# Per-engine step orders for attention and mLSTM, bfloat16 maxima written by their own reductions, and two additions taken from two tensors, in a three-stage decoder layer

## The chip, the cores and the metric

The kernel runs on one core of one Trainium2 chip. The metric is the device time of one execution in microseconds (us). The profile is of one execution.

## The reference, cut to what matters

Sixteen sequences of 256 positions and 256 features go through three pre-norm sub-layers, each with a residual:

```python
x = x + attn(layernorm(x), W_qkv, W_out)      # 16 heads of 16, causal softmax; W_out enters only as a sum per head
x = x + mlstm(layernorm(x), ctx, ctx, ...)    # 8 heads of 32; gates from [q, k, v]; log-sigmoid cumulative sums
x = x + moe(layernorm(x), router, up, down)   # 8 experts of 1024, two per token, exact GELU
```

The softmax subtracts a row maximum, `exp(s - m)`. Any m that is the same for a whole row gives the same result, so m may be rounded. mLSTM computes `S = (q k^T / sqrt(32)) * exp(log_d - max)`, then `S v`, divides by a normalizer, and takes a root-mean-square norm per head.

## The kernel before

Three stages follow each other: attention over 16 batches (to about 320 us), mLSTM over 16 batches (to about 550 us), and the experts in 71 tiles of 128 tokens (to the end). All synchronization is by semaphores. Each engine runs one in-order stream of instructions, written by its own function (`tensor_attn`, `vector_attn`, `scalar_attn`, `gpsimd_attn`, `sync_attn`, and the same five for mLSTM). SyncE (SP) issues nearly all DMAs, in order, and a wait in front of one DMA holds all later ones.

**Attention.** One generator, `attn_steps`, gives all five engines the same list of named steps. In round i it works on several batches at once. In the order of TensorE: S1(i,0) (scores of the upper query half, 4 heads at a time, for the maxima), T0(i-1,0) (transposed scores minus the maximum, for the softmax), PV(i-2), S1(i,1), QK(i+1) (projection of queries and keys), T0(i-1,1), S0(i), VX(i) (values of batch i and transposes of the attention output of i-3), T2(i-1), A4(i-2) (transposes of the output), AX(i) (transposes of the normalized rows: of i+2 for attention and of i-4 for mLSTM's queries), MG(i) (transposes of the maxima, and the gate sums of i-5). VectorE's parts: `tensor_reduce` over each PSUM pair for the maxima (L1049, L1054), Mp (L1062 and L1064: the float32 maxima `mxn` split into a bfloat16 high part and a bfloat16 rest), A4 (L1073 to L1077), AX (L1085 the low part of the mLSTM queries, L1090 the low part of xn), MG (L1103, the gate sums). ScalarE's parts: exponentials of T0 (L1354) and T2 (L1360), the copies of QK (L1372 to L1374), A6c (L1419, the context's high part), AX (L1430, L1391), MG (L1395, the transposed maxima). GpSimd's: the causal selects (L1548), the layer norm's power of -0.5 (L1522), the weight splits (L1531, L1533: a float32 chunk in `STG` is split into two bfloat16 parts), and A6c (L1579).

PSUM is used as four pairs of banks, given out in TensorE's order: a step waits until the step four places before it has been read out (`pair_free`). So T0's two halves wait for the read-outs of AX and MG, S1's second half for that of A4, S0's second half for that of QK.

The weight chunks: SyncE loads two 128x512 chunks in each round into the two buffers of `STG`, GpSimd splits them. A load waits for the split of the chunk two before it. In SyncE's list a round has loads, A4 (output rows to `o_scr`, then a wait until they have landed, then the load `Mm` from there), AX (`q_scr`, and the next context `CnT`).

In round 15 ScalarE also works on the gates of batches 0 to 7 (GT: a load of another activation table, two copies, a logarithm), VectorE scans them (Gs) and splits them (Gp), and SyncE stores them (Go), loads queries, and loads `LR` (decays), with which mLSTM starts.

**mLSTM.** Here each engine already has its own order, the strings of `ORDER`, in words `kind:lag:unit`: in round i the step is done for batch i-lag. D (decay exponents) and S (scores) come in three units; VectorE's S (L1159) multiplies the two, after ScalarE's exponential (L1439). PV multiplies by the values. B3 to B6, B4x, B5s, B5n, B4o normalize, add the residual, take the third layer norm, and compute router logits (L890); R1 to R6 route two batches together. `rest` are the attention's steps of the last batches and the second half of the gates. ScalarE and GpSimd also split two weight chunks in a round (L1450, L1586), and `sc` are GpSimd's indirect DMAs that scatter rows (L1610). TensorE's B6 shares a PSUM bank with B4, and waits until VectorE's B4 (L1185 to L1188) has read it.

Two small VectorE operations take a constant as an immediate: L1004, variance plus 1e-5 in every layer norm, and L1212, `8 - KM` in R2.

Of the kernel before, what the change touches and what calls it, by code (L numbers as in the profile page):

```python
# [31 lines left out]
C_ID, C_MASK, C_U, C_SEL, C_M0, C_M1, C_TOK, C_EK, C_J, C_DUMP, C_RB, C_S0, C_IN, C_DN, C_END = (  # L32
    0, 128, 256, 384, 416, 417, 418, 450, 458, 529, 530, 538, 540, 544, 552)
# [40 lines left out]
def attn_steps():  # L74


    for i in range(-2, B + 1):
        if ok(i):
            yield "load", 2 * i, 0
            yield "load", 2 * i + 1, 0  # L80
            yield "S1", i, 0
        if ok(i - 1):
            yield "T0", i - 1, 0
        if ok(i - 2):
            yield "PV", i - 2, 0
        if ok(i + 2):
            yield "A0s", i + 2, 0
        if ok(i):
            yield "S1", i, 1
            yield "split", 2 * i, 0  # L90
        if ok(i + 2):
            yield "A0n", i + 2, 0
        if ok(i + 1):
            yield "QK", i + 1, 0
        if i == B:
            yield "queries", 0, 0
            yield "Gp", 0, 0
            yield "Go", 0, 0
            yield "decays", 0, 0
        if ok(i - 4):  # L100
            yield "A6s", i - 4, 0
        if i == -2:
            yield "weights", 0, 0
        if ok(i - 1):
            yield "T0", i - 1, 1
        if ok(i):
            yield "S0", i, 0
            yield "split", 2 * i + 1, 0
        if ok(i) or ok(i - 3):
            yield "VX", i, 0  # L110
        if ok(i - 4):
            yield "A6n", i - 4, 0
        if ok(i - 1):
            yield "T2", i - 1, 0
        if ok(i):
            yield "Mp", i, 0
        if i == B - 1:
            yield "GT", 0, 0
        if ok(i - 4):
            yield "A6c", i - 4, 0  # L120
        if ok(i - 2):
            yield "A4", i - 2, 0
        if i == B - 1:
            yield "Gs", 0, 0
        if ok(i + 2) or ok(i - 4):
            yield "AX", i, 0
        if ok(i) or ok(i - 5):
            yield "MG", i, 0
        if i == 13:
            yield "Gt", 0, 0  # L130
        if i == -1:
            yield "weights", 1, 0
        if i == 0:
            yield "weights", 2, 0
# [20 lines left out]
def weight_chunks():  # L155
# [19 lines left out]
}  # L175


def entries(engine):

    for word in ORDER[engine].split():  # L180
        kind, lag, *u = word.split(":")
        yield kind, int(lag), int(u[0]) if u else 0


def mlstm_steps(engine):
# [60 lines left out]
def build(nc, x, ctx_in, ctx_t, wqkv, wout, wg, bg, gain, wr, br, wup, wdn, cst, out):  # L246
# [6 lines left out]
    with st:  # L253
# [56 lines left out]
        mxn = sb("mxn", [128, 2, 2, 4, 2], F32, ca)  # L310
# [23 lines left out]
        Mph = Mp[:, :, :, :, 0:4].rearrange("p t a j (r h) -> p (t a j) r h", h=2)  # L334
        mxv = mxn[:, :, :, :, :].rearrange("p t a j r -> p (t a j) r")
# [42 lines left out]
        steps = list(attn_steps())  # L378
# [27 lines left out]
        lns = [s[:2] for s in steps + dve_steps if s[0] in ("A0s", "A6s", "B5s")]  # L406
# [8 lines left out]
        qk = of(steps, "QK")  # L415
        qkm, q_, ke_, ko_ = (sig(n, qk) for n in ("qkm", "q_", "ke_", "ko_"))
        vmm, v_ = sig("vmm", [(b,) for b in range(B)]), sig("v_", [(b,) for b in range(B)])
        s1 = [(b, P, u) for b, P in of(steps, "S1") for u in range(2)]
        s1m, mx1 = sig("s1m", s1), sig("mx1", s1)
        s0 = [(b, u) for b, _ in of(steps, "S0") for u in range(2)]  # L420
        s0m, mx0 = sig("s0m", s0), sig("mx0", s0)
        each = [(b,) for b in range(B)]
        mp_, mpT, mt_ = (sig(n, each) for n in ("mp_", "mpT", "mt_"))
        t0m, ex0, pt0 = (sig(n, [(b, P, u) for b, P in of(steps, "T0") for u in range(2)]) for n in ("t0m", "ex0", "pt0"))
        t2m, ex2, pt2 = (sig(n, [(b, u) for b, _ in of(steps, "T2") for u in range(2)]) for n in ("t2m", "ex2", "pt2"))
# [8 lines left out]
        for kind, b, P in steps:  # L434
# [183 lines left out]
        def tensor_attn(e, w):  # L618
            for kind, b, P in steps:
# [370 lines left out]
        def ln_stats(e, w, kind, b):  # L990
# [13 lines left out]
            e.tensor_scalar(mv[:, :, 2], mv[:, :, 1], 1e-5, None, ALU.add).then_inc(var.sem, 1)  # L1004
# [31 lines left out]
        def vector_attn(e, w):  # L1036
            for kind, b, P in steps:
# [8 lines left out]
                elif kind == "S1":  # L1046
                    for u in range(2):
                        w.wait_ge(s1m.sem, s1m.at(b, P, u))
                        e.tensor_reduce(mxn[:, 1, P, 2 * u:2 * u + 2, :], pair_of("S1", b, P, u)[:, :, :].rearrange("p j (r c) -> p j r c", r=2),  # L1049
                                        AX.X, ALU.max, negate=True).then_inc(mx1.sem, 1)  # L1050
                elif kind == "S0":
                    for u in range(2):
                        w.wait_ge(s0m.sem, s0m.at(b, u))
                        e.tensor_reduce(mxn[:, 0, :, 2 * u:2 * u + 2, :].rearrange("p a j r -> p j a r"),  # L1054
                                        pair_of("S0", b, u)[:, :, :].rearrange("p j (a r c) -> p j a r c", a=2, r=2),
                                        AX.X, ALU.max, negate=True).then_inc(mx0.sem, 1)
                elif kind == "Mp":
                    w.wait_ge(mx1.sem, mx1.at(b, 1, 1))
                    w.wait_ge(mx0.sem, mx0.at(b, 1))
                    w.wait_ge(mpT.sem, mpT.at(b - 1))  # L1060
                    w.wait_ge(p_init.sem, p_init.at("Mp0"))
                    e.tensor_copy(Mph[:, :, :, 0], mxv).then_inc(dvc.sem, dvc.up())  # L1062
                    w.wait_ge(dvc.sem, dvc.n)
                    e.tensor_tensor(Mph[:, :, :, 1], mxv, Mph[:, :, :, 0], ALU.subtract).then_inc(mp_.sem, 1)  # L1064
# [77 lines left out]
        def vector_mlstm(e, w, experts):  # L1142
# [9 lines left out]
            for kind, b, u in dve_steps:  # L1152
# [58 lines left out]
                elif kind == "R2":  # L1211
                    e.tensor_scalar(XB[:, t0:t0 + 4, 259], KM, -1.0, 8.0, ALU.mult, ALU.add)  # L1212
# [125 lines left out]
        def scalar_attn(e, w):  # L1338
            for kind, b, P in steps:
# [195 lines left out]
        def gpsimd_attn(e, w):  # L1535
# [15 lines left out]
            for kind, b, P in steps:  # L1551
# [111 lines left out]
        def sync_attn(e, w):  # L1663
# [25 lines left out]
            for kind, b, P in steps:  # L1689
# [165 lines left out]
def constants():  # L1855
# [16 lines left out]
    c[:, C_S0] = p % 32 < 2  # L1872
    c[:, C_S0 + 1] = (p % 32 == 2) | (p % 32 == 3)
# [3 lines left out]
    c[:, C_DUMP] = TOK + p  # L1877
    c[:, C_RB:C_RB + 8] = REG * np.arange(8)
# [32 lines left out]
```

## Time and profile before

| | |
|---|---|
| Median of three runs | 974.06 us (972.89 to 978.18) |
| Profiled execution | 972.35 us, span 970.6 us |
| Busy share | TensorE 91%, VectorE 63%, GpSimd 52%, ScalarE 51% |
| Mean granted TensorE clock | 0.965 of 2.4 GHz |

Lines of a timeline give the start, the length, the engine, the line, the operation with its output and inputs, how many were merged, and in brackets how long the engine had been idle and who released it. Matmuls are pipelined, so the next may begin before the end that is printed.

### The profile page before, as it was taken

To read this page: it belongs to the slowest core of one execution; us is meant where nothing else is said; L and a number is where in the kernel's file an instruction comes from. 1 tells how busy PE (TensorE), PEld (TensorE's weight loads), DVE (VectorE), ACT (ScalarE), POOL (GpSimd) and SP (SyncE) were. 2 spreads that over 40 slices of the span, in tenths; PEclk is the share of its full clock that TensorE was granted. 3 is DMA by queue.
4 is the path that set the end of the run, shared out by engine and by line. 5 is a ranking of instruction groups with operands and counts; after the bars stand their busy time and mean duration, and the time that the engine had idled before them with its cause. 6 is when DMAs were issued, how large, how long until landed. Compare 5 with 4: busy or idle time off the path is not lost.

```text
span 970.6 us, 31715 instructions
## 1 busy us (share of the span) xinstructions
PE 880.4 (91%) x11877; PEld 652.7 (67%) x11966; DVE 616.0 (63%) x1324; ACT 490.8 (51%) x839; POOL 501.4 (52%) x705
## 2 busy tenths in 40 slices
PE   4899999989997688999998998999999999999995
PEld 3566666766765445556665776878787878778783
DVE  4766776676767455679898677555555555555552
ACT  3566767767765556556664643333333333333331
POOL 2454756665665433357777677633444434444432
PEclk9899999999998988889998999999999999999998
DMA  8213343334244654355564433433232333233222
GB/s 273 66 24 88 84 112 113 80 89 140 78 88 138 131 174 146 101 160 177 186 193 134 122 73 91 99 67 51 47 51 46 53 49 51 46 51 51 46 35 23
DMA packets 133198, 92.97 MB, mean 96 GB/s; under 512 B 75712, under 2 KB 114112, under 8 KB 132928
## 3 DMA queue, kind: packets, MB, share of 16 engines
q1 hardware_dynamic: 119760, 73.10, 27.2%
q0 software_dynamic: 13296, 17.83, 11.2%
q8 instruction: 106, 1.74, 0.7%
q14 instruction: 36, 0.29, 0.1%
HBM read 54.65 MB, written 37.32 MB: 95 GB/s over the span
## 4 chain that ended last, share of the span: by engine, by line
PE 63%; DVE 11%; ACT 7%; DMA 6%; issue 4%; POOL 3%; SPq 3%; POOLq 0%; DVEq 0%; ACTq 0%
PE pair L963 19%; PE pair L977 10%; PE pair L979 7%; PE pair L665 4%; PE pair L687 3%; PE pair L701 3%; DMA o_scr<-On 3%; DMA STG<-wup_in 2%; PE pair L840 2%; PE pair L638 2%; ACT PT L1360 2%; PE pair L714 2%; PE pair L854 2%; DVE SD L1159 2%; PE pair L929 1%
## 5 line engine op out<-in xcount | busy, mean ns | idle before, releaser
L963 PE MATMUL pair<-XTs,WU 128*128 128x128 bf16 x3408 | 284.0, 219 | 7.7 <-DVE XTs L1303 4.0
L963 PEld LDWEIGHTS pair<-XTs,WU 128*128 x3408 | 237.7, 98 | 75.4 <-issue 12.2
L1637 POOL DMA_INDIRECT out_d<-XB x71 | 115.6, 1629 | 202.5 <-DVE XB L1325 168.8
L1503 ACT ACTIVATE Hf<-pair 128x512 f32<-128x512 f32 x142 | 84.9, 598 | 217.2 <-PE pair L963 217.0
L977 PE MATMUL pair<-WD,Hh 128*128 x479 | 181.1, 379 | 0.2
L1316 DVE CAST Hh<-Hf 128x512 bf16<-128x512 f32 x142 | 64.3, 453 | 164.5 <-ACT Hf L1503 160.2
L979 PE MATMUL pair<-WD,Hl 128*128 x568 | 154.8, 272 | 4.8
L1548 POOL TENSOR_SCALAR_AFFINE_SELECT PT<-PT 128x512 f32<-128x512 f32 (+1 forms) x96 | 74.7, 793 | 56.8 <-ACT PT L1354 52.0
L1318 DVE TENSOR_TENSOR Hl<-Hf,Hh 128x512 bf16<-128x512 f32 x142 | 99.7, 702 | 4.9
L1049 DVE TENSOR_REDUCE mxn<-pair 128x4 f32<-128x1024 f32 x64 | 75.2, 1216 | 27.4 <-PE pair L646 27.3
L1610 POOL DMA_INDIRECT xs_scr<-XB,WGf x64 | 68.6, 1071 | 28.2 <-issue 16.7
L665 PE MATMUL pair<-Q,K 32*128 32x128 f32 (+1 forms) x1024 | 66.3, 360 | 17.3 <-DVE Gq L1103 10.6
L1354 ACT ACTIVATE PT<-pair 128x1024 f32<-128x1024 f32 x64 | 62.2, 1029 | 37.4 <-PE pair L670 37.4
L1159 DVE TENSOR_TENSOR SD<-pair,SD 128x1024 f32<-128x1024 f32 x48 | 58.6, 1221 | 19.9 <-PE pair L840 19.8
L1439 ACT ACTIVATE SD<-pair 128x1024 f32<-128x1024 f32 x48 | 49.0, 1020 | 43.4 <-PE pair L823 43.4
L665 PEld LDWEIGHTS pair<-Q,K 32*128 32x128 f32 x1024 | 42.4, 189 | 30.9 <-ACT MT L1395 19.5
L1586 POOL TENSOR_TENSOR WD<-STG,WD 128x512 bf16<-128x512 f32 x32 | 37.5, 1182 | 43.8 <-ACT WD L1450 43.6
L1054 DVE TENSOR_REDUCE mxn<-pair 128x8 f32<-128x1024 f32 x32 | 37.7, 1219 | 32.4 <-PE pair L646 32.4
L977 PEld LDWEIGHTS pair<-WD,Hh 128*128 128x128 bf16 x568 | 55.5, 98 | 2.5 <-issue 0.8
L979 PEld LDWEIGHTS pair<-WD,Hl 128*128 128x128 bf16 x568 | 55.5, 98 | 0.1
L1510 ACT ACTIVATE yt<-pair,ix 128x256 f32<-128x256 f32 x71 | 33.7, 474 | 39.7 <-PE pair L979 39.6
L1623 POOL TENSOR_SCALAR ix<-XB,TE 128x1 f32<-128x1 f32 x55 | 52.8, 960 | 0.0
(245 smaller groups left out, 1756.5 us busy)
## 6 DMA issues: line engine op xcount, KB each, us to landing
XB<-xs_scr SPq DMA_DIRECT2D x71, 130.0 KB, 2.1
STG<-wup_in SPq DMA_DIRECT2D x32, 256.0 KB, 4.7
q_scr<-SPL SPq DMA_DIRECT2D x16, 512.0 KB, 4.2
STG<-wdn_in SPq DMA_DIRECT2D x32, 256.0 KB, 3.0
o_scr<-On SPq DMA_DIRECT2D x32, 128.0 KB, 4.1
Mm<-o_scr SPq DMA_DIRECT2D x16, 256.0 KB, 2.9
CnT<-ctxt_in SPq DMA_DIRECT2D x16, 256.0 KB, 4.5
CX<-ctx_in SPq DMA_DIRECT2D x16, 256.0 KB, 3.9
```

The costliest lines, as they stand in the source:

```text
L665: e.matmul(o, K[rows, r, par, a, k0:k0 + 128], Q[rows, r, a, 256 - wd:256], start=True, stop=False, skip_group_check=True)
L963: t = e.matmul(upb(j, k)[:, 128 * (fm % 4):128 * (fm % 4) + 128], WU[:, bass.ds(reg[j] * 4096 + off, 128)], XTs[:, r, hx, dk, :], start=n ...
L977: e.matmul(yb[r][:, 0:512], Hh[:, r, hsl], WD[:, bass.ds(reg[i] * 4096 + 512 * fk, 512)], start=fk == 0, stop=False, skip_group_check=True)
L979: t = e.matmul(yb[r][:, 0:256], Hl[:, r, hsl], WD[:, bass.ds(reg[i] * 4096 + 512 * fk, 256)], start=False, stop=fk == 7, skip_group_check= ...
L1049: e.tensor_reduce(mxn[:, 1, P, 2 * u:2 * u + 2, :], pair_of("S1", b, P, u)[:, :, :].rearrange("p j (r c) -> p j r c", r=2), AX.X, ALU.max, ...
L1159: e.tensor_tensor(SD[:, un % 3, :, :], ZS[:, :, :].rearrange("p g (a c) -> p (g a) c", a=2), SD[:, un % 3, :, :], ALU.mult).then_inc(sd_.s ...
L1316: e.tensor_copy(Hh[:, r, hs], Hf[:, r, hs]).then_inc(hhi.sem, 1)
L1318: e.tensor_tensor(Hl[:, r, hs], Hf[:, r, hs], Hh[:, r, hs], ALU.subtract).then_inc(hlo.sem, 1)
L1503: e.activation(Hf[:, r, hs], upb(j, k), ACT.Gelu).then_inc(gel.sem, 1)
L1548: e.affine_select(out=dg, in_=dg, pattern=[[0, n], [1, 128]], compare_op=ALU.is_ge, fill=0.0, base=0, channel_multiplier=-1).then_inc(done ...
L1610: e.indirect_dma_start(out=xs, out_offset=bass.IndirectOffsetOnAxis(ap=SLI[:, m % 2, k, tt:tt + 1], axis=0), in_=XB[:, 4 * m + tt, :], in_ ...
L1637: e.indirect_dma_start(out=out, out_offset=bass.IndirectOffsetOnAxis(ap=XS[:, i % NX, 256:257].bitcast(I32), axis=0), in_=Yf[:, i % NY, :] ...
```

## The change

- Attention gets orders of its own for each engine, `ROUND`, read by `attn_steps(engine)` with the words of `ORDER`. `LIMITS` gives the batches of each step.
- `mxn` and the step Mp are gone. The reductions write bfloat16 maxima straight into `Mp` (one value for each head instead of a high and a low one); VectorE's S1 waits for the transposes of the batch before, TensorE's MG for the reductions, and TensorE's PV also for the selects of T0.
- mLSTM gets new orders.
- L1004 and L1212 become `tensor_tensor` with a constant column of `CF`.

```diff
-def attn_steps():      # one list for all engines
+ROUND = {
+    "tensor": "AX:1 MG:1 S1:0:0 T0:1:0 PV:2 S1:0:1 QK:-1 T0:1:1 S0:0 VX:0 T2:1 GT:15 weights:0:2 A4:2",
+    "vector": "Gp:16 weights:-2:0 A6s:4 weights:-1:1 S1:0:1 S0:0 VX:0 A4:2 weights:0:2 MG:0 AX:0 S1:-1:0 Gs:15 A0s:-3",
+    "scalar": "PV:2 A0n:-2 QK:-1 T0:1:1 Gt:13 A6c:4 weights:-2:0 A6n:4 VX:0 T2:1 weights:-1:1 AX:0 GT:15 MG:0 T0:0:0",
+    "gpsimd": "split:0 T0:1:0 T0:1:1 split:0 GT:15 T2:1 weights:0:2 A6c:4 A0s:-3 A6s:3",
+    "sync": "GT:15 load:0 A4:3 AX:1 Go:16 queries:16 decays:16",
+}
...
 ORDER = {
-    "tensor": "D:0:0 B6:4 R4:5 PV:1:1 S:0:0 D:0:1 PV:1:2 rest:0:0 D:0:2 S:0:1 rest:0:1 B5:3 PV:0:0 rest:0:2 B4:1 S:0:2",
-    "vector": "S:0:0 rest:0:0 B5s:2 S:0:1 R2:4 rest:0:1 rest:0:2 B4:1 first:14 R3:4 S:0:2 R1:3 R5:4 R6:4 B4x:1",
-    "scalar": "D:0:0 rest:0:2 split:0 D:0:1 B3:1 rest:0:0 split:0 rest:0:1 split:0 R1:4 B5:3 D:0:2 B5n:2 B4p:1",
-    "gpsimd": "sc:0 B4p:2 sc:0 R6:5 sc:0 split:0 split:0 B5s:2 rest:0:0 rest:0:1 rest:0:2 split:0",
-    "sync": "load:0 B1:0:1 B1:-1:0 B4o:2 rest:0:2 rest:0:0 rest:0:1 row:15",
+    "tensor": "D:0:0 B6:4 R4:5 PV:1:1 S:0:0 rest:0:0 D:0:1 PV:1:2 rest:0:1 D:0:2 B5:3 S:0:1 PV:0:0 rest:0:2 B4:1 S:0:2",
+    "vector": "B4x:2 rest:0:0 S:0:0 R5:5 R6:5 rest:0:1 B5s:2 S:0:1 rest:0:2 R2:4 B4:1 first:14 R3:4 S:0:2 R1:3",
+    "scalar": "rest:0:2 split:0 B4p:2 D:0:0 B5n:3 split:0 rest:0:0 D:0:1 rest:0:1 split:0 R1:4 B3:1 B5:3 D:0:2",
+    "gpsimd": "B4p:2 rest:0:0 sc:0 R6:5 split:0 split:0 sc:0 rest:0:1 sc:0 split:0 rest:0:2 B5s:2",
+    "sync": "load:0 rest:0:2 B1:0:1 B1:-1:0 rest:0:0 B4o:2 rest:0:1 row:15",
 }
...
-            e.tensor_scalar(mv[:, :, 2], mv[:, :, 1], 1e-5, None, ALU.add)
+            e.tensor_tensor(mv[:, :, 2], mv[:, :, 1], CF[:, C_EP:C_EP + 1].broadcast_to([128, 2]), ALU.add)
...
                 elif kind == "S1":
+                    w.wait_ge(mpT.sem, mpT.at(b - 1))
                     for u in range(2):
                         w.wait_ge(s1m.sem, s1m.at(b, P, u))
-                        e.tensor_reduce(mxn[:, 1, P, 2 * u:2 * u + 2, :], ...
+                        e.tensor_reduce(Mph[:, 1, P, 2 * u:2 * u + 2, :], ...
...
-                elif kind == "Mp":
-                    e.tensor_copy(Mph[:, :, :, 0], mxv)
-                    e.tensor_tensor(Mph[:, :, :, 1], mxv, Mph[:, :, :, 0], ALU.subtract)
...
-                    e.tensor_scalar(XB[:, t0:t0 + 4, 259], KM, -1.0, 8.0, ALU.mult, ALU.add)
+                    e.tensor_tensor(XB[:, t0:t0 + 4, 259], CF[:, C_EK:C_EK + 1].broadcast_to([128, 4]), KM, ALU.subtract)
```

## Rows read from the trace of the kernel before

**Rows 1.** One stretch of mLSTM: busy us of each engine with instructions, granted clock, DMA share, GB/s.

```profile
398.00:548.00 150.00, 139.93 (x1974) 91.12 (x1974) 125.42 (x332) 90.17 (x175) 96.60 (x151) 0.93 0.53 161
```

**Rows 2.** TensorE's waits from 60 to 287 us: total us, times, longest.

```profile
PE pair L665 <- DVE Gq L1103: 9.9, 9, 1.6
PE pair L665 <- DVE xTl L1090: 1.6, 3, 1.3
```

**Rows 3.** TensorE's timeline at the end of one attention round.

```profile
211.75 0.75 PE L791 MATMUL pair<-WGs,SPL 128*128 128x16 bf16 x24
...
214.34 0.71 PE L665 MATMUL pair<-Q,K 32*128 32x256 f32 x8 [1.04 <-DVE Gq L1103]
```

**Rows 4.** VectorE's timeline in the same stretch.

```profile
209.92 1.25 DVE L1064 TENSOR_TENSOR Mp<-mxn,Mp 128x32 bf16<-128x32 f32 x1
...
212.80 0.69 DVE L1085 TENSOR_TENSOR SPL<-pair,SPL 128x512 bf16<-128x512 f32 x1 [0.45 <-ACT SPL L1430]
213.41 0.68 DVE L1090 TENSOR_TENSOR xTl<-pair,xTh 128x512 bf16<-128x512 f32 x1
```

**Rows 5.** TensorE's timeline where attention starts up.

```profile
30.78 0.67 PE L625 MATMUL pair<-OTs 128*128 128x256 f32 x2 [1.53 <-issue]
...
33.85 1.24 PE L665 MATMUL pair<-Q,K 32*128 32x256 f32 x8 [0.62 <-DVE wsq L1033]
```

**Rows 6.** The chain that ended last, from 290 us.

```profile
291.85 5.55 DMA STG<-wup_in
...
301.69 1.82 ACT PT L1360 x2
303.53 1.28 ACT L1406
...
315.54 3.16 DMA g_scr<-pp
```

**Rows 7.** SyncE's queue after the gates: issues.

```profile
311.15 0.91 SPq L1735 DMA_DIRECT2D WD<-q_scr  x1
...
314.87 1.28 SPq L1723 DMA_DIRECT2D g_scr<-pp  x2
318.77 0.34 SPq L1748 DMA_DIRECT2D LR<-g_scr  x1
```

**Rows 8.** TensorE's timeline: the first mLSTM batches and the second half of the gates.

```profile
343.20 1.08 PE L906 MATMUL pair<-CF,Mm 128*128 128x128 f32 x4 [4.98 <-DMA Mm<-o_scr]
...
380.69 1.09 PE L881 MATMUL pair<-CF,XB 128*128 128x128 f32 x4 [2.11 <-ACT r L1408]
...
416.28 0.84 PE L840 MATMUL pair<-Q 64*128 64x128 bf16 x24 [1.81 <-DVE SD L1159]
```

**Rows 9.** TensorE's waits from 400 to 550 us.

```profile
PE pair L890 <- DVE sm L1188: 3.0, 5, 1.0
PE pair L854 <- DMA CX<-ctx_in: 1.3, 1, 1.3
```

**Rows 10.** VectorE's two operations with an immediate: duration min, median, max.

```profile
L1004 DVE TENSOR_SCALAR LS<-LS x48: 168/169/2483, 5.5 to 564.5; 128x2 f32<-128x2 f32 x48
L1212 DVE TENSOR_SCALAR XB<-WGf x8: 159/1166/2806, 416.1 to 585.4; 128x4 f32<-128x4 f32 x8
```

**Rows 11.** L1212 beside GpSimd, and an operation of two tensors beside GpSimd.

```profile
486.97 2.28 POOL L1586 TENSOR_TENSOR WD<-STG,WD 128x512 bf16<-128x512 f32 x2
487.11 2.17 DVE L1212 TENSOR_SCALAR XB<-WGf 128x4 f32<-128x4 f32 x1
...
540.15 1.16 POOL L1586 TENSOR_TENSOR WD<-STG,WD 128x512 bf16<-128x512 f32 x1
540.17 1.19 DVE L1219 TENSOR_TENSOR CF<-CF 128x32 f32<-128x32 f32 x1
```

**Rows 12.** Two stretches at a lower granted clock; columns as in the first group.

```profile
380.00:398.00 18.00, 17.31 (x146) 10.93 (x148) 7.99 (x18) 7.22 (x15) 2.77 (x8) 0.53 0.30 92
469.00:472.50 3.50, 3.50 (x42) 1.47 (x38) 3.29 (x7) 0.66 (x2) 1.81 (x3) 0.56 0.65 199
```

More of the change, by code:

```diff
@@ L71, in ok @@
     return 0 <= b < B
-def attn_steps():
[L77 to L134, printed above, removed]
@@ new lines, with words, attn_steps @@
+ROUND = {
[5 rows of a table added]
+}
+LIMITS = {"S1": (0, B - 1), "T0": (0, B - 1), "PV": (0, B - 2), "A0s": (0, B - 1), "A0n": (0, B - 1), "QK": (0, B - 1), "A6s": (0, B - 4),
+          "A6n": (0, B - 4), "S0": (0, B - 1), "VX": (0, B), "T2": (0, B - 1), "A6c": (0, B - 4), "A4": (0, B - 2), "AX": (-2, B), "MG": (0, B)}
+def words(line):
+    for word in line.split():
+        kind, lag, *u = word.split(":")
+        yield kind, int(lag), int(u[0]) if u else 0
+def attn_steps(engine):
+    parts = 0
+    for i in range(-4, B + 3):
+        for kind, lag, u in words(ROUND[engine]):
+            b = i - lag
+            if kind == "load":
+                if ok(b):
+                    yield kind, 2 * b, 0
+                    yield kind, 2 * b + 1, 0
+            elif kind == "split":
+                if ok(b):
+                    yield kind, parts, 0
+                    parts += 1
+            elif kind not in LIMITS:
+                if b == 0:
+                    yield kind, u, 0
+            elif LIMITS[kind][0] <= b <= LIMITS[kind][1]:
+                yield kind, b, u
@@ L169 @@
 ORDER = {
[5 rows of a table removed]
-}
[L178 to L182, printed above, removed]
[5 rows of a table added]
+}
 def mlstm_steps(engine):
@@ L190, in mlstm_steps @@
     for i in range(B):
-        for kind, lag, u in entries(engine):
+        for kind, lag, u in words(ORDER[engine]):
             b = i - lag
@@ L376, in build @@
         Hf = sb("Hf", [128, 2, 1024], F32)
-        steps = list(attn_steps())
+        pe_attn, dve_attn, act_attn, pool_attn, sp_attn = (list(attn_steps(n)) for n in ROUND)
         pe_steps, dve_steps, act_steps, pool_steps, sp_steps = (list(mlstm_steps(n)) for n in ORDER)
@@ L403, in chunk @@
             return src[:, 512 * k:512 * k + 512], v[:, :, 0, :], v[:, :, 1, :], STG[:, c % 2, :].rearrange("p (a w) -> p a w", w=width)
-        lns = [s[:2] for s in steps + dve_steps if s[0] in ("A0s", "A6s", "B5s")]
+        lns = [s[:2] for s in dve_attn + dve_steps if s[0] in ("A0s", "A6s", "B5s")]
         LNK = {k: i % 4 for i, k in enumerate(lns)}
@@ L433, in build @@
         users = []
-        for kind, b, P in steps:
+        for kind, b, P in pe_attn:
             if kind in ("S1", "T0"):
@@ L618, in tensor_attn @@
         def tensor_attn(e, w):
-            for kind, b, P in steps:
+            for kind, b, P in pe_attn:
                 if kind == "weights" and b == 2:
@@ L1003, in ln_stats @@
             w.wait_ge(dvc.sem, dvc.n)
-            e.tensor_scalar(mv[:, :, 2], mv[:, :, 1], 1e-5, None, ALU.add).then_inc(var.sem, 1)
+            e.tensor_tensor(mv[:, :, 2], mv[:, :, 1], CF[:, C_EP:C_EP + 1].broadcast_to([128, 2]), ALU.add).then_inc(var.sem, 1)
         def vector_setup(e, w):
@@ L1036, in vector_attn @@
         def vector_attn(e, w):
-            for kind, b, P in steps:
+            for kind, b, P in dve_attn:
                 if kind == "weights":
@@ L1338, in scalar_attn @@
         def scalar_attn(e, w):
-            for kind, b, P in steps:
+            for kind, b, P in act_attn:
                 if kind == "weights" and b < 2:
@@ L1549, in causal @@
                                 channel_multiplier=-1).then_inc(done.sem, 1)
-            for kind, b, P in steps:
+            for kind, b, P in pool_attn:
                 if kind == "weights" and b == 2:
@@ L1688, in sync_attn @@
                             onesb[:, :].rearrange("p (a c) -> p a c", a=1).broadcast_to([128, 2, 128])).then_inc(l_on, 16)
-            for kind, b, P in steps:
+            for kind, b, P in sp_attn:
                 if kind == "load":
```

41 lines of the change are left out of this document (18 added, 23 removed).

## The prediction

> **What bounds the kernel now.** I read the page first: TensorE is busy for nine tenths of the span, so only its gaps, its slow stretches, and whatever lengthens them can be won. Then the windows by stage: in the long mLSTM stretch of 150 us VectorE is busy 125 and TensorE 140 [rows 1], so there VectorE is nearly a second bound. Then TensorE's waits and the timeline in front of each. In the attention rounds from 60 to 287 us there is one regular hole, in front of T0, nine times and 9.9 us in all, released by the last of VectorE's read-outs [rows 2]. The reader is to see in the timeline that TensorE has finished its gate sums at 212.50 and S1 by about 213.3, and begins T0 at 214.34 after 1.04 us of nothing [rows 3], because VectorE started L1085 only at 212.80, waiting for ScalarE, and then had two more operations to do [rows 4]. Between the stages the chain of waits is a queue: weight load, GpSimd's split, normalized rows, exponentials, table load, gates, then SyncE's issues [rows 6, 7], and TensorE ends it with a wait of 4.98 us for a DMA [rows 8]. In mLSTM it waits 3.0 us for VectorE's B4 and 1.3 for a context load [rows 9], and twice around the gates' second half [rows 8]. The expert stage is untouched.
>
> **The change part by part**, against the profiled execution of 972.35 us, which lies 1.7 below the median of the runs.
>
> *The steady attention rounds.* TensorE's cyclic order stays the same: AX and MG are only written at the head of the next round. What moves is who reads out. ScalarE does A6c before the exponentials of T2 instead of between them and AX, so L1430 comes about 0.5 us earlier, and VectorE's L1085 no longer waits for it. VectorE loses the step Mp (its second operation took 1.25 us in this round [rows 4]), but it was in front of A4, which TensorE feeds only at about 210.8, so most of that was slack. VectorE now does the gate sums first: they can begin when TensorE's end, at 212.50 [rows 3]. I give them 0.13 us (an estimate: the old order left 0.61 from L1085 to L1090, and 0.25 between the end of L1090 at 214.09 and T0, the sums among it [rows 3, 4]). Then L1085 starts at 212.63 instead of 212.80, and T0 follows after 1.54 less the 0.11 that the sums no longer take at the end: 214.06. The hole goes from 1.04 to 0.76. It doesn't close, because the three operations still stand in one row behind TensorE's gate sums. Nine holes of 0.76 instead of 9.9 us: 3.1. The one round with a wait of 1.3 for L1090 [rows 2] goes to 0.76 too, and one wait of 0.3 for a late normalized row goes with the earlier splits: **-4.0 us**. Bounds: 0, if the row is held elsewhere; -11.5, if all holes close.
>
> The reductions' bfloat16 output I cost at nothing: L1085 and L1090 write bfloat16 from PSUM in 0.69 and 0.68 us for 512 columns [rows 4], the pace of any read from PSUM there. S1's new wait for the transposes is free: they end before 212, and S1 starts behind L1090. PV's wait for the selects of T0 is free since the select of T2 comes later on the same engine.
>
> *The start.* The sum over W_out (weights 2) moves ahead of AX(0) and MG(0) on TensorE. It waits for a GpSimd memset behind two weight splits, until 30.78 [rows 5], in either order, so AX, MG and S1 now come behind it. T0 stood at 33.85 [rows 5]; I get 34.6 from a matmul group of 0.9, transposes of 0.8 and VectorE's part behind the sums. Against +0.75 stands 0.35 in the next round, where QK's copies no longer stand behind a late xn: **+0.4 us** (0 to +2).
>
> *The end of attention.* SyncE now issues round i's loads in front of A4(i-2), not behind its output DMA, and GpSimd does the norm's power ahead of the splits. In round 15 the load of 5.55 us began at 291.85 and held the split, then the power, the row QN and only then the exponentials at 301.69 [rows 6]. TensorE had T2 ready at 299.1, so they can start 2.6 earlier. The table load at 303.53 [rows 6] now follows AX instead of preceding it, so the logarithm gains only 1.4 to 1.8, but VectorE starts its scans at once, and the split of the gates ends at about 311.7. SyncE issues the gates first (1.3 us) and the queries then (311.15 to 314.87 before, 3.7 us) where it was the reverse [rows 7]. The gates' landing of 3.16 [rows 6] is hidden behind the queries: the first LR issue goes from 318.77 [rows 7] to 311.7 + 1.3 + 3.7 = 316.7. All of SyncE's queue behind it (A4(14), Mm, the contexts, LR of the next batch, and the Mm that TensorE waits 4.98 for [rows 8]) is back to back and shifts as one: **-2.1 us** (0 to -3).
>
> *mLSTM, the two additions.* L1212 needs 0.16 us and took up to 2.8; it took 2.17 where it began beside two of GpSimd's subtractions, together 2.28, and it ended with them. An operation of two tensors that began beside one such subtraction ended with that one: 1.19 [rows 11]. So I take 1.2 as the worst for both new additions, where L1004's worst was 2.48 and L1212's 2.81 [rows 10]. L1212 stands in front of B4, and TensorE's waits for B4 sum to 3.0 in five [rows 9]; four of them, 2.7 us, lie behind an L1212 that took 2.2 or 2.8 and are shorter than the 1.0 to 1.6 it gives back: -2.7. Behind the two longer ones TensorE's granted clock fell for a stretch such as 469.0 to 472.5, at 0.56 [rows 12]; half speed costs 0.44 of 3.5 us each, on a busy TensorE 1.5 to 1.7: -3.3.
>
> *mLSTM, the orders.* The splits now come before most of the scatter DMAs on GpSimd, so the last loads and the context behind them start earlier: the wait of 1.3 [rows 9] goes. In round 3 ScalarE does the hyperbolic tangent before D's second exponential, and TensorE has GT before D's third unit; the wait that ended at 380.69 [rows 8] is replaced by three shorter ones in front of B5 and PV, and I get PV 1.0 earlier. In round 5 VectorE's Gp, some 3.9 us, stands before S's first unit instead of behind it: the wait of 1.81 at 416.28 [rows 8] becomes one of 3.9 in front of S's second unit, partly given back: +1.0. R1's exponential ahead of B3 (0.25 us) lies in 0.5 of slack before PV. B5n behind D's first exponential frees ScalarE where it waited for GpSimd, but no TensorE wait hangs on that. Together: -2.7 - 3.3 - 1.3 - 1.0 + 1.0 = **-7.3 us** (+6 to -16; the lower end if the 18 us at a clock of 0.53 [rows 12] also return to full, which is worth 8).
>
> Sum: -4.0 + 0.4 - 2.1 - 7.3 = -13.0; 972.35 - 13.0 = 959.4, and as the median lies above the profiled execution, **960 us**.
>
> A rule that speaks against the additions: the Trainium skill, "SBUF — State Buffer", section "Who interferes with whom", says that a VectorE instruction with two SBUF inputs contends with a GpSimd instruction that reads SBUF, and that `tensor_tensor` has no 2-port mode but contends in this way. By it both new forms still wait behind GpSimd's subtraction; the trace agrees for one of them (the row with 1.19). By the rule alone nothing would be gained there, which is the second rival below.
>
> **The rivals.**
>
> *The clock comes back too.* With fewer holes around the gates' second half, the stretch of 18 us at 0.53 [rows 12] stays at full clock or halves. For it: two holes of 1.4 and 2.1 us stand right in front of it. Against it: I only shorten them to three of about 1. Worth 4 to 8: 953.
>
> *The additions gain nothing.* They have two SBUF inputs and can be held by the same subtractions, even by both of two if each new one wins; new orders also put other operations beside them. Without -2.7 and -3.3: 966.
>
> *Slower: ScalarE's first split.* It now stands ahead of B4p and D's first exponential at the head of each round, and waits for a weight chunk from a load that SyncE may issue only after GpSimd's split of two chunks before. Before, it came after D. If the chunk lands more than about 2 us after the last exponential of the round, D's first exponential, S and D's second unit all slide. For it: VectorE and TensorE have only 5 to 15% of slack there [rows 1]. Against: GpSimd splits earlier as well. At 1.5 us in each of some 12 rounds: +18 - 1, so 977.
>
> *Nothing measurable.* The holes only move: the row behind the gate sums and SyncE's queue give back what is won, and round 5's hole costs a slow stretch. 971.
>
> **How the numbers follow.** Forecast 0.48 (its own range 955 to 965), the clock too 0.18, additions without gain 0.17, nothing 0.09, slower 0.08. The range 948 to 970 reaches from the clock's lower end to the additions' upper and leaves out the last two. A measurement of this kernel can tell about 0.5%, 969.2 to 978.9. Faster is the first three, less a little for their upper edges: 0.81; the same 0.12; slower 0.07.
>
> **What would show it.** T0's hole near 0.75 with L1090 as its releaser; no 5 us of GpSimd waiting for STG in the attention rounds; exponentials of T2 in round 15 right behind TensorE; the first LR issue about 6 us earlier than 318.77 (2.1 and the rounds before); L1004 and L1212 never above 1.3; TensorE's wait for B4 gone; a wait near 4 us in front of S in round 5. Wrong would be: a hole of T0 that stays at 1.04 or vanishes, waits of ScalarE for STG in front of B4p, or more slow stretches than before.

## The result and the profile after

The changed kernel takes 949.62 us (median of four runs, 947.91 to 955.48) against 973.47 for the kernel before: a ratio of 0.9757, 95% interval 0.9728 to 0.9786. The forecast was 960 with a range of 948 to 970. The profiled execution of the changed kernel takes 950.63 us, span 948.8; of before 972.35, span 970.6. The difference of the spans, 21.8 us, is what I divide up.

The page of the changed kernel, busy time by engine, then the granted clock in 40 slices:

```profile
PE 869.4 (92%) x11877; PEld 647.8 (68%) x11966; DVE 588.0 (62%) x1292; ACT 488.6 (51%) x839; POOL 497.3 (52%) x705
...
PEclk9899999999998979999999999999999999999998
```

**The attention rounds.** TensorE's waits from 60 to 283 us, then its timeline and VectorE's at the end of the round that answers to [rows 3, 4]:

```profile
PE pair L634 <- DVE xTl L1055: 7.6, 12, 0.7
```

```profile
208.94 0.75 PE L762 MATMUL pair<-WGs,SPL 128*128 128x16 bf16 x24
...
211.22 0.71 PE L634 MATMUL pair<-Q,K 32*128 32x256 f32 x8 [0.73 <-DVE xTl L1055]
```

```profile
208.05 0.37 DVE L1038 RECIPROCAL pair<-pair 128x32 f32<-128x32 f32 x1 [1.45 <-PE pair L702]
...
209.73 0.19 DVE L1068 TENSOR_TENSOR Gq<-pair,BG 128x32 f32<-128x32 f32 x1 [0.37 <-PE pair L762]
209.84 0.68 DVE L1050 TENSOR_TENSOR SPL<-pair,SPL 128x512 bf16<-128x512 f32 x1
210.44 0.68 DVE L1055 TENSOR_TENSOR xTl<-pair,xTh 128x512 bf16<-128x512 f32 x1
```

The hole in front of T0 is 0.73 us where it was 1.04 [rows 2, 3], and the low part of xn (now L1055) ends it. From S1 of the first full round to S1 of the last (65.90 to 285.59 before, 66.28 to 281.57 after) the rounds give 4.4 us; the start costs 0.4.

**Between the stages.** The chain that ended last, and SyncE's issues:

```profile
294.49 1.92 ACT PT L1325 x2
296.41 0.54 ACT SPL L1395
296.96 1.28 ACT L1371
...
304.87 0.29 DVE pp L1098
305.18 0.62 SPq L1688
```

```profile
305.18 1.28 SPq L1688 DMA_DIRECT2D g_scr<-pp  x2
306.55 0.55 SPq L1700 DMA_DIRECT2D WD<-q_scr  x1
307.15 1.84 SPq L1702 DMA_DIRECT2D WD<-q_scr  x4
309.10 0.33 SPq L1713 DMA_DIRECT2D LR<-g_scr  x1
```

In the attention rounds GpSimd no longer waits for STG at all, where it waited 47.7 us in twelve. The STG load of 5.55 us and everything that it held [rows 6] are off the chain: the exponentials of T2 run 7.2 us earlier, the table load 6.6, the first LR issue 9.7 (318.77 [rows 7] to 309.10).

**mLSTM.** TensorE's three waits that answer to [rows 8], in order: the load Mm, the second half of the gates, and round 5. Then its waits from 390 to 535 us, for [rows 9], and R2's first operation, for [rows 10]:

```profile
334.65 1.09 PE L877 MATMUL pair<-CF,Mm 128*128 128x128 f32 x4 [5.17 <-DMA Mm<-o_scr]
...
372.24 0.63 PE L852 MATMUL pair<-CF,XB 128*128 128x128 f32 x4 [1.11 <-ACT r L1373]
...
398.46 1.46 PE L811 MATMUL pair<-Q 64*128 64x256 bf16 x12 [2.51 <-DVE SD L1124]
```

```profile
PE pair L811 <- DVE SD L1124: 5.6, 3, 2.5
PE pair L934 <- issue: 1.1, 1, 1.1
```

```profile
L975 DVE TENSOR_TENSOR LS<-LS,CF x48: 161/164/1607, 5.6 to 542.7; 128x2 f32<-128x2 f32 x48
L1177 DVE TENSOR_TENSOR XB<-CF,WGf x8: 148/151/157, 401.2 to 563.6; 128x4 f32<-128x4 f32 x8
```

No wait for B4 is left, R2's operation (L1212 before, L1177 now) never takes above 0.157 us, and the wait of the context load is gone. The windows from the end of the wait for Mm to the first expert matmul, first before, then after (us, then busy us and instructions of each engine, granted clock, DMA share, GB/s):

```profile
343.20:548.56 205.36, 189.08 (x2622) 122.13 (x2623) 156.43 (x395) 123.01 (x233) 113.98 (x181) 0.89 0.51 157
```

```profile
334.65:526.68 192.03, 177.98 (x2622) 115.93 (x2623) 146.10 (x395) 123.47 (x233) 112.53 (x181) 0.96 0.53 166
372.00:390.00 18.00, 17.22 (x244) 11.62 (x244) 11.97 (x26) 12.29 (x27) 5.11 (x11) 1.00 0.37 112
```

mLSTM takes 13.3 us less. The same 2622 matmuls are busy for 178.0 us instead of 189.1, at a mean granted clock of 0.96 instead of 0.89: 11.1 us are shorter busy time, 2.2 fewer gaps. The stretch that stood at 0.53 [rows 12] is at 1.00. In windows of 1 us, the stretches of this stage below 0.8 add up to some 44 us before (380 to 397 [rows 12] and five others) and to some 15 after (334.65 to 343, 398 to 401, 510 to 514). The account of the spans: -4.4 rounds, +0.4 start, -4.5 end of attention (the wait for Mm ends 8.55 earlier, 4.0 of it from the rounds and the start), -13.3 mLSTM, nothing in the expert stage.

### The profile page after: what moved, and what is told of

Read it like the earlier page. It is cut to its first block, busy times and chain, and to the rows that moved or that the text cites. A ratio compares the mean times of both kernels' runs of the same rounds, so it can differ in the third digit from the quotient of the medians.

```text
span 948.8 us, 31667 instructions
## 1 busy us (share of the span) xinstructions
PE 869.4 (92%) x11877; PEld 647.8 (68%) x11966; DVE 588.0 (62%) x1292; ACT 488.6 (51%) x839; POOL 497.3 (52%) x705
## 4 chain that ended last, share of the span: by engine, by line
PE 78%; DVE 8%; ACT 6%; issue 3%; DMA 2%; SPq 2%; POOL 0%; ACTq 0%; DVEq 0%; POOLq 0%
PE pair L934 19%; PE pair L948 10%; PE pair L950 7%; PE pair L634 5%; PE pair L671 5%; PE pair L657 4%; PE pair L811 3%; PE pair L607 3%; PE pair L684 2%; PE pair L825 2%; PE pair L837 2%; PE pair L900 2%; ACT SD L1404 1%; PE pair L786 1%; PE pair L861 1%
## 5 line engine op out<-in xcount | busy, mean ns | idle before, releaser
L1487 POOL TENSOR_TENSOR LS<-LS,mhalf 128x2 f32<-128x2 f32 x48 | 34.4, 716 | 95.7 <-DVE LS L975 95.3
L1022 DVE TENSOR_REDUCE Mp<-pair 128x4 bf16<-128x1024 f32 x64 | 75.2, 1216 | 13.0 <-PE pair L615 12.7
L1575 POOL DMA_INDIRECT xs_scr<-XB,WGf x64 | 66.0, 1032 | 32.4 <-issue 17.3
L1027 DVE TENSOR_REDUCE Mp<-pair 128x8 bf16<-128x1024 f32 x32 | 37.7, 1219 | 45.1 <-PE pair L615 45.1
```

The source lines that it names most:

```text
L1022: e.tensor_reduce(Mph[:, 1, P, 2 * u:2 * u + 2, :], pair_of("S1", b, P, u)[:, :, :].rearrange("p j (r c) -> p j r c", r=2), AX.X, ALU.max, ...
L1575: e.indirect_dma_start(out=xs, out_offset=bass.IndirectOffsetOnAxis(ap=SLI[:, m % 2, k, tt:tt + 1], axis=0), in_=XB[:, 4 * m + tt, :], in_ ...
```

## The experiments

Changes below are against the kernel that is named. Each kernel was timed beside the kernel before (973.81 to 975.25 us in these series), not beside the changed kernel, so a difference of 1 or 2 us from its 949.62 says nothing.

### Run 1: the additions alone, in the kernel before

```diff
-            e.tensor_scalar(mv[:, :, 2], mv[:, :, 1], 1e-5, None, ALU.add)
+            e.tensor_tensor(mv[:, :, 2], mv[:, :, 1], CF[:, C_EP:C_EP + 1].broadcast_to([128, 2]), ALU.add)
-                    e.tensor_scalar(XB[:, t0:t0 + 4, 259], KM, -1.0, 8.0, ALU.mult, ALU.add)
+                    e.tensor_tensor(XB[:, t0:t0 + 4, 259], CF[:, C_EK:C_EK + 1].broadcast_to([128, 4]), KM, ALU.subtract)
```

> The kernel before with only the two additions written as operations of two tensors, the old orders kept. My theory: L1212 gives back 1.0 to 1.6 us behind four waits for B4 (2.7 us) and two stretches at a lower granted clock go with them (3.3 us): 973.5 - 6 = 967.5 us, both operations never above 1.3 us, TensorE's waits for B4 near 0.3 us in sum. Rival (the additions gain nothing, since two SBUF inputs wait behind the same subtractions): 973.5 us, and operations that still take up to 2.8 us.

Measured: 975.92 us, ratio 1.0004 (0.998 to 1.0027). The two lines over the whole span, then R2's operation beside GpSimd's pair of subtractions:

```profile
L1004 DVE TENSOR_TENSOR LS<-LS,CF x48: 161/164/2470, 5.5 to 567.9; 128x2 f32<-128x2 f32 x48
L1212 DVE TENSOR_TENSOR XB<-CF,WGf x8: 151/1288/2793, 416.0 to 588.7; 128x4 f32<-128x4 f32 x8
```

```profile
488.11 2.33 DVE L1212 TENSOR_TENSOR XB<-CF,WGf 128x4 f32<-128x4 f32 x1
...
488.13 2.28 POOL L1586 TENSOR_TENSOR WD<-STG,WD 128x512 bf16<-128x512 f32 x2
```

The reader is to see two ends: 490.44 and 490.41. The new form is held through both subtractions as the old one was [rows 11]. The rival is right, my bound of 1.2 us was wrong, and the interval leaves no room for the 6 us.

### Run 2: the additions undone, in the changed kernel

> The changed kernel with only the two additions back as operations with an immediate. If they are worth about 6 us in the new orders too: 949.6 + 6 = 955.6 us, with some of them above 2 us and TensorE waiting for B4 behind them. If the new orders alone had put R2 away from GpSimd's subtractions, or if the old form costs nothing there: 949.6 us.

Measured: 950.81 us (946.72 to 954.82), and the immediate form of R2's operation takes 0.154 to 0.164 us. So in neither order are the additions worth anything that can be measured, and what took R2 out of its delay is an order.

### Run 3: the old mLSTM orders, in the changed kernel

> The changed kernel with the old mLSTM orders, its attention part and its two additions kept. From the two traces attention is 8.1 us shorter up to the last context load. If that is all of attention's share and the additions are worth 6 us: 973.5 - 8.1 - 6 = 959.4 us, and TensorE's long stretch at a lower granted clock around the second half of the gates is back. Rival, the orders of mLSTM gain nothing and the clock came back with the additions: about 950 us. Rival, the additions gain nothing: 965.4 us.

Measured: 967.09 us, ratio to before 0.9921 (0.9896 to 0.9946). So the new attention alone makes the kernel 6.7 us faster, and the mLSTM orders on top of it give 16.3 to 17.5 (967.09 against 950.81 of run 2 and 949.62). Windows of the same stretch of mLSTM, and of a slow part in it:

```profile
333.87:543.31 209.44, 192.32 (x2622) 125.12 (x2623) 155.06 (x395) 122.30 (x231) 113.77 (x182) 0.88 0.50 155
372.00:382.00 10.00, 8.32 (x62) 5.92 (x62) 3.43 (x10) 4.85 (x10) 2.59 (x8) 0.54 0.20 60
```

The low clock behind the gates' second half comes back with the old orders, and so do the waits for B4 (2.7 us in four) and for the context load (3.2 us). Attention's gain doesn't arrive whole: the wait for Mm ends 9.3 us earlier than in the kernel before (333.87, 343.20), but with the same orders mLSTM then takes 209.4 us where it took 205.4.

### Runs 5 to 8: which engine's order

Runs 5 to 7 take the changed kernel and put back the old `ORDER` string of one engine (run 6 those of two, TensorE and ScalarE), and run 8 puts GpSimd's new string alone into the kernel before.

```diff
# 5
-    "gpsimd": "B4p:2 rest:0:0 sc:0 R6:5 split:0 split:0 sc:0 rest:0:1 sc:0 split:0 rest:0:2 B5s:2",
+    "gpsimd": "sc:0 B4p:2 sc:0 R6:5 sc:0 split:0 split:0 B5s:2 rest:0:0 rest:0:1 rest:0:2 split:0",
# 6
-    "tensor": ... (new)     "scalar": "rest:0:2 split:0 B4p:2 D:0:0 B5n:3 split:0 rest:0:0 D:0:1 ..."
+    "tensor": ... (old)     "scalar": "D:0:0 rest:0:2 split:0 D:0:1 B3:1 rest:0:0 split:0 ... B5n:2 B4p:1"
# 7
-    "vector": "B4x:2 rest:0:0 S:0:0 R5:5 R6:5 rest:0:1 B5s:2 S:0:1 rest:0:2 R2:4 B4:1 ..."
+    "vector": "S:0:0 rest:0:0 B5s:2 S:0:1 R2:4 rest:0:1 rest:0:2 B4:1 ... R1:3 R5:4 R6:4 B4x:1"
```

> The changed kernel with GpSimd's old mLSTM order. In the profiles so far R2's small operation ends together with GpSimd's pair of weight subtractions in either form, and in the changed kernel it stands beside a scatter DMA instead. Theory: it is GpSimd's order that took it out from beside the subtractions, and the four delays of 2.2 to 2.8 us with TensorE's waits for B4 (2.7 us) and two slow stretches (3.3 us) come back: 949.6 + 6 = 955.6 us. Rival, the whole 17.5 us of the mLSTM orders hang on it: about 967 us. Rival, VectorE's or ScalarE's order did it: 949.6 us, and L1177 stays at 0.16 us.

> The changed kernel with the old mLSTM orders of TensorE and ScalarE (the second half of the gates after D's second exponential, and ScalarE's first split after D). Theory: the hole of 2.1 us and a granted clock of 0.5 for 17 us around 375 to 392 us come back, worth 1 + 8 us: 958.6 us. Rival, the clock there was chance or hangs on the other orders: about 950 us. Rival, ScalarE's early split costs: faster than 949.6 us.

> The changed kernel with VectorE's old mLSTM order (Gp behind S's first unit, R5, R6 and B4x at the end of a round, R2 one step earlier). By my prediction's term for round 5 this is 1 us better, 948.6 us, and the wait of 2.51 us in front of S's second unit becomes one near 1.8. Rival: R2 now begins beside GpSimd's work or B4 comes late behind it, and TensorE waits for VectorE again: 953 us or more.

> The kernel before with GpSimd's new mLSTM order alone. If that order is what frees R2: no R2 above 0.2 us, TensorE's waits for B4 gone, and 973.5 - 6 = 967.5 us. If what it gives elsewhere too (earlier loads, context) is most of the gain: below 962 us. If it only works with the other engines' new orders: 973.5 us.

| kernel | us | against 949.62 | R2's operation, longest |
|---|---|---|---|
| 5: GpSimd's old | 976.43 | +26.8 | 2.878 us |
| 6: TensorE's and ScalarE's old | 993.71 | +44.1 | 0.675 us |
| 7: VectorE's old | 959.19 | +9.6 | 0.159 us |
| 8: before with GpSimd's new | 986.58 (ratio 1.0117, 1.0088 to 1.0146) | | 0.681 us |

GpSimd's order does free R2 (runs 5 and 8), but nearly every number that I expected is far off: the orders aren't a sum of parts. Runs 5 and 6 are slower than all five old strings together (967.09), and run 8 is slower than the kernel before. In run 5 the rows of three engines show what is late; GpSimd, SyncE, ScalarE, and ScalarE's waits from 400 to 530 us:

```profile
455.99 2.27 POOL L1551 TENSOR_TENSOR WD<-STG,WD 128x512 bf16<-128x512 f32 x2
```

```profile
457.18 1.45 SPq L1616 DMA_DIRECT2D STG<-wdn_in  x2
```

```profile
460.88 0.63 ACT L1415 ACTIVATE WD<-STG 128x512 bf16<-128x512 f32 x1 [6.23 <-DMA STG<-wdn_in]
461.42 0.20 ACT L1426 ACTIVATE sm<-sm 128x16 f32<-128x16 f32 x1
461.65 0.22 ACT L1428 ACTIVATE sm<-sm 128x16 f32<-128x16 f32 x1
461.78 1.01 ACT L1404 ACTIVATE SD<-pair 128x1024 f32<-128x1024 f32 x1
```

```profile
ACT WD L1415 <- DMA STG<-wdn_in: 50.2, 11, 6.4
```

GpSimd's subtractions, late as in the old order, let SyncE reload the two buffers only at 457.18; ScalarE, whose split now stands first, waits 6.23 us for that chunk, and B4p and D's exponential behind it come late. From 335 to 560 us TensorE then waits 8.7 us for D's exponential, 6.4 for the copy of the normalizer's input (L1422) and 5.4 for B4, in the changed kernel 3.1, 1.3 and 0. It is the slower rival of my prediction, and in the changed kernel it is there too, as 13.3 us in eight waits (longest 4.10), which TensorE hardly notices. In run 6 it is the other way round; the waits of GpSimd and of ScalarE, 400 to 530 us:

```profile
POOL WD L1551 <- ACT WD L1415: 25.2, 14, 6.7
```

```profile
ACT XB L1300 <- POOL LS L1490: 38.1, 8, 6.3
```

GpSimd subtracts early and waits for ScalarE's high part, which is late, so its norms come late, and ScalarE waits for those: a ring. From 335 to 560 us TensorE waits 13.4 us for S and 13.2 for D's exponential (5.6 and 3.1 in the changed kernel). Run 8 shows the same pair (24.9 and 38.0 us). In run 7 TensorE waits 10.3 us in seven for S; I put that down to B4x, R5 and R6 at the end of VectorE's round, which weren't moved singly.

Run 6 also answers my question on the clock. The hole in front of the second half of the gates is back, as long as in [rows 8], and the clock behind it stays whole:

```profile
380.91 0.63 PE L852 MATMUL pair<-CF,XB 128*128 128x128 f32 x4 [2.11 <-ACT r L1373]
```

```profile
380.91:398.00 17.09, 16.98 (x238) 11.79 (x238) 11.52 (x25) 12.00 (x23) 5.41 (x14) 1.00 0.44 129
```

So that hole alone doesn't bring the stretch of [rows 12]. (Of the two holes that my prediction names there, the first is 0.60 us here, where it was 1.42.) The slow stretches of run 6 stand elsewhere (362 to 372 at 0.51, 406 to 424 at 0.53).

### Run 9: R2's operation moved, in the kernel before

```diff
# R1
                     link(e.tensor_reduce(KM, KY, AX.X, ALU.max))
+                    e.tensor_scalar(XB[:, t0:t0 + 4, 259], KM, -1.0, 8.0, ALU.mult, ALU.add)
                     link(e.tensor_tensor(O1, KY, bt(KM), ALU.is_equal))
# R2
-                    e.tensor_scalar(XB[:, t0:t0 + 4, 259], KM, -1.0, 8.0, ALU.mult, ALU.add)
```

> The kernel before with L1212 alone moved: still the form with an immediate, but at the end of R1, some 5 us earlier, where GpSimd does small operations and scatters and no weight subtraction. Theory: the delay belongs to this operation wherever it starts beside the subtractions, so it takes 0.16 us now, the later operations of R2 follow without delay, and my term of 2.7 + 3.3 us comes: 967.5 us. Rival, the next small operation of R2 (the sum at L1214) is held in its place: no change, 973.5 us. Rival, the delays vanish but were slack that TensorE takes elsewhere: 971 to 973 us.

Measured: 974.14 us, ratio 0.9971 (0.994 to 1.0001). What was L1212's place, twice: beside a pair of subtractions, and beside one.

```profile
486.24 0.18 DVE L1214 TENSOR_REDUCE WGf<-CF 128x4 f32<-128x32 f32 x1
486.33 2.72 DVE L1215 SCALAR_TENSOR_TENSOR CF<-CF 128x32 f32<-128x32 f32 x1
...
538.96 0.18 DVE L1214 TENSOR_REDUCE WGf<-CF 128x4 f32<-128x32 f32 x1 [1.45 <-ACT CF L1474]
539.06 1.03 DVE L1215 SCALAR_TENSOR_TENSOR CF<-CF 128x32 f32<-128x32 f32 x1
```

```profile
486.71 2.29 POOL L1586 TENSOR_TENSOR WD<-STG,WD 128x512 bf16<-128x512 f32 x2
...
538.89 1.16 POOL L1586 TENSOR_TENSOR WD<-STG,WD 128x512 bf16<-128x512 f32 x1 [0.16 <-ACT WD L1450]
```

The delay has only passed to another operation of R2: not to the reduction at L1214, which runs inside a subtraction in 0.18 us, but to L1215, whose two inputs are both in SBUF. It ends with the subtraction in both cases. The Trainium skill, "SBUF — State Buffer", section "Who interferes with whom", says that on this chip reductions never contend with GpSimd, and that an instruction with two SBUF inputs contends with a GpSimd instruction that reads SBUF; the trace agrees with both (0.18 and 1.03 us). My prediction cited that rule and set it aside.

### Run 10: the maxima in two parts again, in the changed kernel

The float32 `mxn` and the step Mp return, in front of VectorE's A4; TensorE's MG waits for it.

> The changed kernel with the maxima as before: float32 from the reductions, then a step on VectorE (in front of A4) that splits them into a high and a low bfloat16 part, on which TensorE's transposes wait. My prediction costed the removal of that step as slack: VectorE idles 1.45 us in front of A4, the step takes some 1.5 to 1.9 us, and 0.37 us of idle time follow behind A4: 949.6 us, hole in front of T0 still 0.73. Rival, the 4.4 us that the steady rounds gained come from this removal: 954 us and a hole near 1.0.

Measured: 950.11 us (947.09 to 955.34). From S1 of the first full round to that of the last it takes 215.3 us, as the changed kernel does, with the hole at 0.74. VectorE's idle time in front of A4 shrinks from 1.45 to 0.78 and pays for the step. So the bfloat16 maxima are worth nothing in time that can be measured, in the new order. There the step is also shorter, 0.72 us in two operations (0.49 and 0.23): in the kernel before it was 0.56 and 1.25, and the second one lay beside a subtraction of GpSimd (209.91 to 211.08) and ended 0.09 us behind it.

### Runs 4, 11 and 12: the order behind the gate sums, and two further versions

```diff
-    "vector": "... A4:2 weights:0:2 MG:0 AX:0 S1:-1:0 ..."
+    "vector": "... A4:2 weights:0:2 AX:0 MG:0 S1:-1:0 ..."
# the two later versions also: T0 and T2 on TensorE
-                    for u in range(2):
-                        pair_free(w, kind, *key, u)
+                    pair_free(w, kind, *key, 0)
...
+                            if g == 0 and j == 2:
+                                pair_free(w, kind, *key, 1)
# the last also
-    "vector": "B4x:2 rest:0:0 S:0:0 ..."
+    "vector": "B4x:2 S:0:0 rest:0:0 ..."
```

> The changed kernel with VectorE's read-outs at the end of an attention round in the old order: first the two low parts, then the gate sums. In the profile of the changed kernel the first low part can start when ScalarE's high part of the queries ends, about 0.4 us before it starts now, because it now stands behind the gate sums, which wait for TensorE. If that holds, the hole in front of T0 goes from 0.73 to about 0.45 us and the gate sums release it, in some 10 to 13 rounds: 949.6 - 3 = 946.6 us. Rival, the row is held by ScalarE's part or by TensorE's gate sums either way: hole 0.7, 949.6 us. It would also say that this piece of the change was a loss.

> The changed kernel with the low parts ahead of the gate sums on VectorE, as in the earlier run, and TensorE's T0 and T2 waiting for their second pair only in front of the third matmul. The low part of xn then ends at about 210.74 where it ended at 211.12, and T0's first half needs only that: a hole of about 0.35 instead of 0.73, in ten rounds and more: 949.6 - 4 = 945.6 us. The earlier run (hole 0.52, but 954.9 us) shows that mLSTM can give this back by slow stretches of the granted clock, so the rival is 950 to 955 us with the attention rounds 4 us shorter all the same.

> The same as the run before it, and VectorE's mLSTM order with the rest (in round 5 the split of the gates' second half, 3.9 us) behind S's first unit. By my prediction's term this takes 1 us off round 5 and perhaps the slow stretch behind the hole of 2.51 us: 944.5 us, with a hole near 1.8 at about 398 us. Rival, the rest of rounds 0 to 3 comes late behind S and mLSTM starts slower: above 946 us.

| version | us (lowest) | ratio to before | rounds, first to last S1 | hole at T0 |
|---|---|---|---|---|
| changed kernel | 949.62 (947.91) | 0.9757 (0.9728 to 0.9786) | 215.3 | 0.73 |
| run 4: low part first | 954.85 (943.57) | 0.9755 (0.9708 to 0.9803) | 213.4 | 0.52 |
| run 11: and second wait later | 951.29 (946.16) | 0.9739 (0.970 to 0.9777) | 212.5 | 0.38 |
| run 12: and gates later | 954.2 (949.81) | 0.9774 (0.9738 to 0.9811) | 212.4 | 0.38 |

Without their longest executions (957.9 and 962.48 us) the medians of runs 4 and 11 are 953.67 and 947.91. The profile of run 11 is of that longest execution, so only its attention rounds are read. T0 in the round of [rows 3], in run 4 and in run 11:

```profile
210.36 0.71 PE L634 MATMUL pair<-Q,K 32*128 32x256 f32 x8 [0.52 <-DVE Gq L1068]
```

```profile
209.88 0.75 PE L635 MATMUL pair<-Q,K 32*128 32x256 f32 x8 [0.38 <-ACT MT L1361]
```

In attention the reasons hold: doing the gate sums first, which my prediction counted as part of the gain, is a loss of 1.9 us against doing them last, since ScalarE's high part is ready before TensorE's gate sums are (209.44 and 209.69 in the changed kernel). The two changes together give 2.8. (ScalarE's MT is the next thing in the row.) But no version's time is distinguishable from the changed kernel's, because mLSTM moves by as much. In run 4, a window behind the same hole of 2.5 us as in the changed kernel, and then the changed kernel's own:

```profile
398.00:412.00 14.00, 13.89 (x116) 9.22 (x118) 7.16 (x26) 3.58 (x7) 4.33 (x9) 0.52 0.48 150
```

```profile
398.00:401.50 3.50, 3.04 (x28) 1.31 (x28) 2.94 (x10) 0.00 (x0) 1.20 (x3) 0.53 0.66 181
```

After one and the same wait the half clock (1.2 of 2.4 GHz) lasts for 3.5 us in one execution and for 14 in another. Nor does a shorter hole give a shorter stretch: in run 12 the hole is 1.10 us and 7 us at 0.53 follow (403 to 410), in run 7 it is 1.11 and 10 us at 0.51 follow (402 to 412). Executions of run 4's kernel range from 943.57 us at a mean clock of 0.984 to 957.41 at 0.969. A few us gained in attention can't be told from that with six runs.

## Why the prediction was right, and where it wasn't

**Steady rounds, -4.0: right.** 4.4 measured, hole at 0.73, released by the low part, and the maxima's split was slack, as run 10 shows. Within it, "VectorE now does the gate sums first" was no gain: by run 4 it took 1.9 back, and what else moved gave 6.3. I take that for ScalarE's earlier A6c, which no run isolates. The profiles fit it: L1430 ended 0.27 us behind TensorE's gate sums (212.77, 212.50), and its successor ends 0.25 ahead of them.

**The start, +0.4: right only as a sum.** T0 of the second batch stands at 50.79 instead of 50.41, but both terms were mis-sized: T0 of the first batch goes from 33.85 to 35.52, 1.7 later where I had 0.75, and the next round gives 1.3 back where I had 0.35. W_out's sum now waits 3.73 us in one hole instead of the shorter waits of [rows 5].

**End of attention, -2.1: right in mechanism, too small.** 4.5 measured, outside my bound of 3. "The split of the gates ends at about 311.7" was mis-sized: it ended at 314.09 before and at 305.16 now, so 4.9 us earlier apart from the 4.0 of the rounds, where I had 2.4. The exponentials begin 3.2 earlier beyond the rounds (I had 2.6) and the logarithm, and with it the scans, 2.6 (I had 1.4 to 1.8). And from the first scan to the last cast VectorE took 8.1 us before and takes 5.8 now: two read-outs (0.85) are no longer between them, and the subtraction behind the scans and two casts, which took 1.42, 0.61 and 0.75 beside GpSimd's subtraction (307.82 to 308.97) and selects (311.09 to 312.64), take 0.42, 0.28 and 0.28 with GpSimd idle. SyncE then needed 3.9 us from the gates' issue to LR, not 5.0. About 1.2 of this was given back before Mm.

**mLSTM, -7.3: the sum fell short (-13.3), and its largest term was false.** The step that failed is "So I take 1.2 as the worst for both new additions", on which -2.7 and -3.3 hung. One row beside a single subtraction told nothing about a pair of them: run 1 measures 0 (ratio 1.0004), with 2.33 to 2.79 us for the new form beside the pairs. The waits for B4 went all the same, from the orders: GpSimd does its subtractions earlier, so R2 no longer stands beside one. L975 still takes 1.61 us at worst, above the 1.3 that I named as a sign. My -1.3 for the context load held (run 3 has the wait again). Around the gates' second half the holes went from 1.42 and 2.11 us to 0.17, 1.11 and 0.44, so 1.8 less where I had 1.0. ScalarE's waits for STG in front of B4p, which I named as a sign of being wrong, did come (13.3 us, 0.9 before), without making TensorE wait as I feared. For round 5 I forecast a wait near 4 us and found 2.51; putting the gates later there cut the hole to 1.10 and gave nothing in time (run 12).

**The clock.** I took it at 3.3 us through the additions and gave 0.18 to its coming back altogether. That rival came true in what it says of the clock: 11.1 of mLSTM's 13.3 us are shorter busy time of the same matmuls. That it comes with the orders is shown (run 3: 0.88, changed: 0.96). The rival's reason, fewer holes around the gates' second half, is not: run 6 has the hole of 2.11 us without the stretch, and run 4 and the changed kernel have one and the same hole with a long and a short one. What sets off a stretch, and what ends it, stays open. How much R2's delay itself was worth to TensorE stays open too: runs 5, 8 and 9 each changed something else beside it.

So the direction is explained and the size was partly luck. Without the 6.0 us of the additions, which bring nothing, my sum would have been 966. It left only 1.3 us for the mLSTM orders, and they bring the 13.3 us of that stage, mostly through the clock. The measured 949.62 lies in the range of 948 to 970 because its lower edge was set for the case that the clock comes back.

## What to carry to other kernels

Engine orders that feed each other in a ring (high part, low part, reload of the buffer, norm) are one change: try them whole, as putting back one or two of the five cost 10 to 44 us where all five gain 17.5. To free a small VectorE operation from GpSimd, move GpSimd's long ones (runs 5 and 8), not the one operation and not its form (runs 9 and 1): the next one with two SBUF inputs takes the delay. Where TensorE is nearly full, split a difference into busy time at the granted clock and gaps before you explain it: here half of the whole gain (11.1 of 21.8 us) is shorter busy time of the same matmuls.

## What the runs showed of the hardware that I had not expected

- A 128x4 operation of VectorE took 2.17 to 2.88 us instead of 0.16 and ended with the second of two back-to-back GpSimd subtractions, with an immediate (before) or with two tensors (runs 1 and 5). A reduction beside a subtraction took 0.18 (run 9), and S, with one input in PSUM, never more than 1.23 in the changed kernel.
- Some operations with two inputs in SBUF began before the subtractions, in run 9 at 486.33 where GpSimd's began at 486.71, and ended with them; a scatter DMA was being issued then. A scatter DMA's issue alone didn't hold such operations: in the changed kernel L1183 and L1184, at 447.87 and 448.09, took 0.19 us each inside one (447.59 to 448.56). Why the earlier ones were held from their start stays open.
- Executions of one and the same kernel (run 4's) differ by 14 us (943.57 to 957.41), and with them the mean granted clock (0.984 to 0.969).
